# Attention turns: heads evicted behind the copy of the logits, root behind the maximum, context copied earlier, q and k by ScalarE

## What is computed

```python
x = x + 0.5 * _L0_ffn_ref(_layernorm(x), gate_up_proj, down_proj, router_w)   # 8 experts, the best 2 of each token
x = x + _L0_attn_ref(_layernorm(x), conv_w, conv_b, wq, bq, ..., proj_w, proj_b)
x = x + 0.5 * _L0_ffn_ref(_layernorm(x), gate_up_proj, down_proj, router_w)

# in _L0_attn_ref
qkv = conv1d(xp, conv_w) + conv_b            # causal, 3 taps, 3 x 64 channels
q, k, v = split(qkv)                          # then blocks of 128 tokens
scores = einsum('bqhk,bshk->bhqs', qh * scale, kh)      # 8 heads of 64
attn = softmax(where(causal, scores, -1e9))
mha_out = einsum('bqhk,hko->bqo', einsum('bhqs,bshk->bqhk', attn, vh), wo) + bo
out = mha_out @ proj_w + proj_b
```

## Time and profile before

| | |
|---|---|
| median of 3 runs | 757.45 us (755.04 to 759.35) |
| the profiled execution | 758.16 us, span 756.4 us |
| first experts, 0 to 255 us | 255 us, PE busy 226.85, DVE 169.14, ACT 156.11 |
| attention, 255 to 545 us | 290 us, PE busy 259.04, DVE 215.47, ACT 217.55, POOL 190.40 |
| second experts and last sums, 545 to 756 us | 211 us, PE busy 179.05, DVE 136.07, ACT 117.60 |
| maxima of the 32 blocks | start from 261.7 to 531.6 us, one each 8.7 us |

### The profile page before, as it was taken

How to read it: one execution, slowest core, us unless ns; L and a number is a source line. 1 busy time by engine, 2 the same in 40 slices (tenths; PEclk the granted TensorE clock), 3 DMA queues, 4 the chain that set the end, 5 groups by cost and what they waited for, 6 DMA issues and landing times. The chain is left out here.

```text
span 756.4 us, 18879 instructions
## 1 busy us (share of the span) xinstructions
PE 664.9 (88%) x5168; PEld 590.6 (78%) x5169; DVE 520.7 (69%) x1829; ACT 491.3 (65%) x1702; POOL 372.7 (49%) x418
## 2 busy tenths in 40 slices
PE   3999799999996699999898989978778999999854
PEld 3986699999993577878787878767557899999743
DVE  6588466666666467787878777858657677777653
ACT  5775566666664278887877868768444566666633
POOL 4200544444424546657787877554545444444500
PEclk9999899999999789999999999999879999999968
DMA  9930345444442211111222221110224543443289
GB/s 307 304 128 10 106 141 151 143 126 133 129 111 83 77 36 36 50 42 52 77 64 64 71 72 60 33 58 22 88 89 122 160 134 120 130 127 125 71 315 351
DMA packets 60424, 85.50 MB, mean 113 GB/s; under 512 B 10032, under 2 KB 46387, under 8 KB 60340
## 3 DMA queue, kind: packets, MB, share of 16 engines
q1 hardware_dynamic: 47332, 49.73, 21.2%
q0 software_dynamic: 13008, 34.69, 14.6%
HBM read 45.77 MB, written 37.44 MB: 110 GB/s over the span
## 5 line engine op out<-in xcount | busy, mean ns | idle before, releaser
L1811 PE MATMUL CC<-w_hi,turned_parts 128*128 x568 | 175.5, 351 | 3.6 <-issue 3.6
L725 POOL DMA_INDIRECT shared<-h_rows,tok_i x71 | 70.2, 988 | 116.4 <-issue 58.9
L1811 PEld LDWEIGHTS CC<-w_hi,turned_parts 128*128 128x128 f32 x568 | 105.4, 193 | 4.4 <-issue 4.3
L742 POOL DMA_INDIRECT y_rows<-shared,y_dest x71 | 70.0, 986 | 76.0 <-DVE y_dest L1349 57.8
L818 ACT ACTIVATE shared<-CC 128x176 f32<-128x176 f32 x142 | 45.2, 319 | 76.1 <-PE CC L1811 70.1
L1811 PE MATMUL CC<-w_lo,turned_parts 128*128 x284 | 93.3, 328 | 0.0
L934 ACT ACTIVATE pr<-SS,nmax 128x128 f32<-128x128 f32 x256 | 90.5, 401 | 0.5 <-DVE nmax L1542 0.5
L758 POOL TENSOR_TENSOR pr<-pr,prec 128x1024 f32<-128x1024 f32 x31 | 58.9, 1901 | 51.4 <-DVE prec L1572 50.2
L789 POOL DMA_INDIRECT h_regions<-h_store,dest x64 | 65.4, 1022 | 34.9 <-DVE dest L1436 18.4
L1330 DVE TENSOR_TENSOR shared<-shared,CC 128x176 f32<-128x176 f32 x142 | 48.0, 338 | 49.4 <-ACT shared L818 28.0
L766 POOL DMA_INDIRECT yg<-y_rows,slot_i x64 | 62.9, 983 | 34.5 <-DMA y_rows<-shared 15.5
(11 more groups left out here) (376 smaller groups left out, 2100.3 us busy)
## 6 DMA issues: line engine op xcount, KB each, us to landing
yg<-h_regions SPq DMA_DIRECT2D x71, 129.0 KB
y_rows<-shared SPq DMA_DIRECT2D x71, 128.0 KB
w_lo<-y_rows SPq DMA_DIRECT2D x9, 512.0 KB, 8.0
x_sb<-in_x_dram SPq DMA_DIRECT2D x8, 512.0 KB, 8.3
out_dram<-x_sb SPq DMA_DIRECT2D x16, 256.0 KB, 6.2
w_hi<-y_rows SPq DMA_DIRECT2D x7, 512.0 KB, 11.8
w_lo<-in_gupT_dram SPq DMA_DIRECT2D x2, 1408.0 KB, 11.1
shared<-tile_oh SPq DMA_DIRECT2D x32, 64.0 KB
```

The source lines that it names most:

```text
L725: pool.indirect_dma_start(out=rows[:, s % RING, 0:D], out_offset=None, in_=h_dram[:, :], in_offset=bass.IndirectOffsetOnAxis(ap=tok_i[:, s ...
L742: pool.indirect_dma_start(out=y_dram[0:TOPK * TOKENS, :], out_offset=bass.IndirectOffsetOnAxis(ap=y_dest[:, s:s + 1], axis=0), in_=y_sb[:, ...
L1811: i = pe.matmul(CC[:, 512 * (u % 2):512 * (u % 2) + GU], rows_part[:, u % 2, c * P:(c + 1) * P], weights, start=(n == 1), stop=(n == 3 * DC))
```

## The change

On DVE the order of a turn changes. The root goes from ahead of the maximum to behind it (up to turn 31). The copy of the context, `context(b)`, moves into `add_context`, between the addition to x and its statistics. The eviction of the head products moves from behind the reciprocal to directly behind the copy of the logits. A pick of four blocks moves from ahead of `add_context` to behind the eviction; smaller picks move behind `add_context`. The copy of q and k moves from DVE to ACT, where it stands behind the copy of `vo` and ahead of that of `hT`. On PE the ranks of a pick of four blocks move from the end of their turn into the next turn, behind the convolution of v and ahead of the scores.

```diff
@@ -863,6 +863,11 @@
                     a.activation(SS[:, :].rearrange("p (h s) -> p h s", s=P), mask_heads[:, :, :], ACT.Copy
                                  ).then_inc(t["exp"], 1)
 
+                def queries(p):
+                    a.wait_ge(t["conv"], 2 * p + 1)
+                    a.activation(qk[p % 2], B[:, 0:2 * P], ACT.Identity, bias=convb_sb[:, 0:1], scale=1.0
+                                 ).then_inc(t["qk"], 1)
+
                 def turned_pair(p):
                     a.wait_ge(t["xT"], 2 * p + 2)
                     a.activation(pair_of_rows(xT_hi, p), two_turned(), ACT.Copy).then_inc(t["xT_hi"], 2)
@@ -880,6 +885,7 @@
                                          scale=arstd[:, q:q + 1]).then_inc(t["normed"], 1)
                         if p == 0:
                             turned_pair(0)
+                            queries(0)
 
                 def turned(i):
                     if i == 0:
@@ -907,6 +913,8 @@
                     if there(i - 1):
                         a.wait_ge(t["vo"], i)
                         a.activation(vo[:, (u - 1) % 2, :], F[:, :], ACT.Copy).then_inc(t["vo_sb"], 1)
+                    if qk_pair(i) is not None:
+                        queries(qk_pair(i))
                     if there(i - POST):
                         b = i - POST
                         a.wait_ge(t["hrT"], b + 1)
@@ -1493,15 +1501,9 @@
                     sums(2, 1, 0)
                     turned_low(-2)
                     sums(3, 1, 1)
-                    queries(0)
                     root_of(moments[:, 1, :, :], 4, 2)
                     sums(4, 1, 0)
                     evict(-1)
-
-                def queries(p):
-                    v.wait_ge(t["conv"], 2 * p + 1)
-                    v.tensor_tensor(qk[p % 2], B[:, 0:2 * P],
-                                    convb_sb[:, 0:1].to_broadcast([P, 2 * P]), ALU.add).then_inc(t["qk"], 1)
 
                 def root(i):
                     root_of(moments[:, (i - 1) % 2, :, :], i - FIRST_RSTD + 1, 1)
@@ -1520,10 +1522,17 @@
                     v.scalar_tensor_tensor(out=shift[:, :], in0=m[:, :, 0], scalar=-1.0, in1=arstd[:, :],
                                            op0=ALU.mult, op1=ALU.mult).then_inc(t["rstd"], more)
 
+                def context(b):
+                    v.wait_ge(t["mha"], b + 1)
+                    v.tensor_tensor(mhaT[:, :], F[:, 0:P], mha_bias[:, 0:1].to_broadcast([P, P]), ALU.add
+                                    ).then_inc(t["mhaT"], 1)
+
                 def add_context(i):
                     b, u = i - 2, i % GROUP
                     v.wait_ge(t["out"], b + 1)
                     st.did(v.tensor_tensor(x_tile(b), x_tile(b), G[:, 0:D], ALU.add))
+                    if there(i - 1):
+                        context(i - 1)
                     st.wait()
                     v.sem_inc(t["res"], 1)
                     st.did(v.bn_stats(astats[:, 1, :], x_tile(b)))
@@ -1533,35 +1542,34 @@
 
                 def turn(i):
                     u = i % GROUP
-                    if qk_pair(i) is not None:
-                        queries(qk_pair(i))
-                    if i > 0 and (there(i + COMBINE - 1) or there(i - 3)):
+                    if i >= TILES and there(i - 3):
                         root(i)
                     if there(i):
                         v.wait_ge(t["scores"], i + 1)
                         v.tensor_reduce(nmax[:, u % 2, :], SS[:, :].rearrange("p (h s) -> p h s", s=P), AX.X, ALU.max,
                                         negate=True).then_inc(t["max"], 1)
-                    if i == 0:
+                    if there(i):
                         root(i)
                     if v_pair(i) is not None:
                         v.wait_ge(t["vhi"], v_pair(i) + 1)
                         v.tensor_tensor(vst_lo[:, :, :].rearrange("p b n -> p (b n)"), B[:, 2 * P:4 * P],
                                         vst_hi[:, :, :].rearrange("p b n -> p (b n)").bitcast(F32), ALU.subtract
                                         ).then_inc(t["qkv"], 1)
-                    if i in PICKS and i <= TILES:
-                        if PICKS[i][1] < 4:
-                            compare(*PICKS[i])
-                        pick(*PICKS[i])
                     if placed(i, False):
                         place(*placed(i, False))
                     if there(i - 2):
                         add_context(i)
+                    if i in PICKS and i <= TILES and PICKS[i][1] < 4:
+                        compare(*PICKS[i])
+                        pick(*PICKS[i])
                     if there(i - POST):
                         copy_logits(i - POST)
-                    if there(i - 1):
-                        v.wait_ge(t["mha"], i)
-                        v.tensor_tensor(mhaT[:, :], F[:, 0:P], mha_bias[:, 0:1].to_broadcast([P, P]), ALU.add
-                                        ).then_inc(t["mhaT"], 1)
+                    if there(i + 1):
+                        evict(i)
+                    if i in PICKS and i <= TILES and PICKS[i][1] == 4:
+                        pick(*PICKS[i])
+                    if there(i - 1) and not there(i - 2):
+                        context(i - 1)
                     if there(i + 3):
                         turned_low(i)
                     if there(i + COMBINE):
@@ -1576,8 +1584,6 @@
                             v.tensor_tensor(pr[:, u % 2, :, :], pr[:, u % 2, :, :],
                                             prec[:, u % 2, :].unsqueeze(2).to_broadcast([P, NH, P]),
                                             ALU.mult).then_inc(t["norm"], 1)
-                    if there(i + 1):
-                        evict(i)
                     if there(i + COMBINE):
                         b = i + COMBINE
                         st.did(v.bn_stats(astats[:, 0, :], x_tile(b)))
@@ -1931,6 +1937,8 @@
                         convolve_qk(qk_pair(i))
                     if i > 0 and v_pair(i) is not None:
                         convolve_v(v_pair(i))
+                    if i - 1 in PICKS and PICKS[i - 1][1] == 4:
+                        ranks(i - 1)
                     if there(i):
                         if i == 0:
                             for half in range(2):
@@ -2011,7 +2019,7 @@
                         for n, (part, weights) in enumerate(((vst_hi, wvo_hi), (vst_hi, wvo_lo), (vst_lo, wvo_hi))):
                             x = pe.matmul(F[:, :], part[:, u % 2, :], weights[:, :], start=(n == 0), stop=(n == 2))
                         x.then_inc(t["vo"], 1)
-                    if i in PICKS and i < TAIL_TURN:
+                    if i in PICKS and i < TAIL_TURN and PICKS[i][1] < 4:
                         ranks(i)
 
                 def ranks(i):
```

## The result

The changed kernel takes 786.12 us (median of 4 runs, 783.79 to 792.24), the kernel before 756.92 on the same chip (755.04 to 759.35). The ratio is 1.0396, with a 95% interval of 1.033 to 1.0463. The forecast was 777, with a range of 764 to 789; the measured time lies inside that range, 1 us above the 770 to 785 that the forecast gave as its own. The profiled execution took 785.68 us with a span of 783.9; before it was 758.16 and 756.4.

A forecast was written before the change was run, and what follows sets the result against it. The prediction took a ring of waits through projection, addition to x, reciprocal and POOL's multiplication as the bound. Added: +12.8 (turns 9 to 24), -1, +3.3, +2, +3, in all +20 on 757.45; forecast 777 us, range 764 to 789.

The forecast's parts named there:

- The ring: Attention turn: transposes, projection, addition to x, DVE's work up to the reciprocal, POOL's multiplication; 7.91 us in an even turn.
- T: Start of PE's transposes in a turn, 2.24 us after DVE's reciprocal in turn 20 and 2.56 in turn 19.
- 6.7 us from the transposes to the reciprocal: Sign of being right, in even turns of the attention: this stretch takes 6.7 us instead of 5.67.
- about 1.1 us for PE G: Sign of being right: DVE waits this long for PE's projection ahead of the addition to x in even turns.
- 8.95, about 9.0: Even turn's forecast length in us: 7.91 plus 0.56 for the eviction and 0.48 for the context's copy.
- "9.0" for the place: Turn with a place: it fits in the remaining wait ahead of the addition to x; 9.0 us against 8.49.
- 8.8: Odd turn's forecast length in us: 8.20 plus 0.61, from 0.56 eviction and 0.25 context copy, less 0.2.
- the 0.2 taken back for an earlier T: Odd turns: 0.2 us deducted because the bank of the convolution of q and k is free earlier.
- Cost 0: Copy of q and k on ACT: 0.39 us expected, fitting ACT's idle time ahead of the transposes' copy.
- 10.9: Pick turn's forecast length in us: 8.8 plus the pick's full 2.13 standing in the ring, against 9.95 before.
- the rival of the lower clock: PE's idle time brings the lower clock oftener: six more such turns, +10 us, 785 to 795; chance 0.13.
- The rival in which it gets faster: PE itself is the bound, earlier work closes its holes: 1.5 us off five pick turns, -7.5, 750; chance 0.07.

The follow-up runs named there:

- a_evict_back: Changed kernel with the eviction of the head products behind the reciprocal again; ratio 1.0151 to the kernel before.
- a_context_back: Changed kernel with the copy of the context behind the copy of the logits again, ahead of the eviction; ratio 1.029 to the kernel before.
- b_queries_act: Kernel before with only the copies of q and k moved from DVE to ACT; ratio 1.0017 to the kernel before.
- a_root_back: Changed kernel with the root ahead of the maximum again; ratio 1.0373 to the kernel before.
- a_experts_in_wait: Changed kernel with the two experts' rows moved from ahead of the reciprocal to just ahead of the addition to x; ratio 1.0335 to the kernel before.
- b_rec_early_root: Kernel before with the experts' rows behind reciprocal and eviction, and the root behind the maximum; ratio 1.0483 to the kernel before.
- b_rec_early: Kernel before with the experts' rows moved behind the reciprocal and the eviction; ratio 1.0478 to the kernel before.
- b_evict_early: Kernel before with only the eviction moved directly behind the copy of the logits, ahead of the context's copy; ratio 1.0401 to the kernel before.

## Why the prediction was right

**The ring.** Right, and shown by a_evict_back and a_context_back: what is put between the addition to x and the reciprocal is paid in full, and taken out again it comes back. T follows the reciprocal of an even turn by 2.24 us in both kernels. "6.7 us from the transposes to the reciprocal" was 6.74, "about 1.1 us for PE G" was 1.11.

**The terms.** "8.95, about 9.0" for the even turn: 8.98. "9.0" for the place: 8.98. "8.8" for the odd turn: 8.96; the part between T and reciprocal grew by 0.83 as forecast (0.81), but of the 0.2 taken back for an earlier T only 0.07 came. In turn 19 T is 439.62, 2.49 us behind the reciprocal, where it was 2.56 before. The operand of the convolution, the low part, stands 1.74 us ahead of the reciprocal in both kernels (415.89 and 417.63, 436.09 and 437.83), as the prediction had it. But the same operand holds T (4.23 us behind it in turns 17 and 19), so the bank that is free earlier gives nothing. "Cost 0" for q and k fits these sums, which leave no room for a cost, but in b_queries_act, without the other parts, the same move made the even turn 0.5 us longer: no run shows why, and none isolates it in the changed kernel.

**The pick.** "10.9" was mis-sized: 10.52. The 2.13 us of the earlier trace rows were read as the pick's own price. What follows its first row there, and POOL beside it (timelines of the kernel before, turn 21):

```profile
443.13 0.17 DVE L1400 TENSOR_REDUCE pick<-oh 128x4 f32<-128x32 f32 x1
443.33 0.42 DVE L1401 TENSOR_TENSOR rank<-pick,erank 128x32 f32<-128x32 f32 x1
...
442.62 0.56 POOL L776 TENSOR_SCALAR shared<-x_sb,arstd,shift 128x256 f32<-128x256 f32 x1
443.17 0.55 POOL L782 TENSOR_SCALAR h_store<-x_sb,arstd,shift 128x256 f32<-128x256 f32 x1
```

In the changed kernel, turn 17, where POOL is not at work on x:

```profile
425.12 0.15 DVE L1407 TENSOR_TENSOR h_store<-y_row,zeros 128x4 f32<-128x4 f32 x1
425.19 0.18 DVE L1408 TENSOR_REDUCE pick<-oh 128x4 f32<-128x32 f32 x1
425.40 0.19 DVE L1409 TENSOR_TENSOR rank<-pick,erank 128x32 f32<-128x32 f32 x1
```

Two of the pick's small operations, that of the earlier trace rows and L1401, took 0.51 and 0.42 us beside POOL's two normalisations, and 0.15 and 0.19 apart from them. Moved, the pick costs 1.55 us (425.12 to 426.67): 8.96 + 1.55 = 10.51. The other pick operations took about the same in both places.

**The sum.** Four turns were forecast at +3.2 and came at +2.9; the odd turn was taken 0.16 us too short and the pick turn 0.38 too long, so part of the agreement is luck. Turns 2 to 8 gave +5.25 (forecast 5.3), turns 9 to 24 +12.4 (11.8), turns 25 to 31 +5.0 (3). The attention is thus 22.7 against 20, and the missing part is mainly in the late turns. Turn 26 took 12.59 us, at a mean granted clock of 0.73, and turn 10 took 11.21 at 0.70, so both ran in part at the lower of PE's two levels (1.2 and 2.4 GHz); both follow a pick turn in which PE had been busy for over 10 us. The windows of turns 10 and 26, and of turn 26 in a_root_back:

```profile
350.55:361.76 11.21, 8.98 (x53) 7.06 (x54) 6.67 (x25) 7.09 (x26) 6.96 (x7) 0.70 0.15 48
504.25:516.84 12.59, 9.03 (x53) 7.17 (x53) 6.82 (x25) 7.09 (x26) 6.89 (x7) 0.73 0.12 43
...
495.96:504.95 8.99, 5.90 (x53) 4.82 (x54) 7.28 (x25) 6.98 (x26) 5.77 (x6) 1.00 0.09 30
```

In the kernel before, the same kind of turn fell to 0.84 and 0.83 (turns 10 and 22) and took 9.59 and 9.61 instead of 8.49. So the two disturbed turns add an estimated (11.21 + 12.59 - 2 x 8.98) - (9.59 + 9.61 - 2 x 8.49) = 3.6 us. That is the rival of the lower clock, in small: not oftener, but deeper. Emptier turns alone did not bring it: turns 14, 18 and 22 are of the same kind, PE was busy for only 5.9 us of each, and the clock was 1.00. And a_root_back, whose turns 16 to 19 are those of the changed kernel within 0.02 us, kept 1.00 in turn 26; its turns 25 to 31 are 65.4 us, only 0.8 above the kernel before, where the changed kernel's are 5.0 above. So most of the extra time in the late turns seems to belong to that one profile and not to a term of the sum. What makes the clock fall in one such turn and not in the next stays open. The rival in which it gets faster counts five pick turns, of which there are six: -9 instead of -7.5 us, which touches nothing else.

**Off by the rest.** The measured difference is 29 us, the turns explain 23. Ahead of turn 1 and behind turn 31 the profile has +2.4 each. Neither is shown to come from the change, by profiles of chips of the same speed. Ahead of turn 1, a_experts_in_wait has the changed kernel's code and took 276.12 us, where the changed kernel took 278.64 and the kernel before 276.21. Behind turn 31, b_rec_early_root and b_rec_early have the code of the kernel before and took 220.9 and 215.9 us, the changed kernel 220.3 and the kernel before 217.9. The sum had no term for these 4.8 us, nor for a deeper fall of the clock. So the turns brought the forecast within 9 us, and it is in part the width of the range that holds 786.

**The rule for the fullest engine.** The Trainium skill, Perfetto Trace Analysis, sections "Identifying the Most-Contended Engine" and "Optimization Strategy", would have one take the engine of the highest occupancy and make what it waits for start sooner. PE was the fullest at 88%. Its context did come earlier (T + 3.48 instead of T + 3.73 in even turns), and so did its heads (T + 4.40 instead of T + 5.79), and the kernel became 4% slower. That rule did not hold here, as the ring said.

## What to carry to other kernels

Where several engines pass one token round, find the ring before moving anything: follow one turn from an instruction back to itself, and sort each engine's work into what lies on that way, which is paid in full, and what lies in a wait, which is free. An early start for a consumer that isn't late is paid by everything queued behind it. Costs of moves don't add, when two of them share a wait. And an instruction's duration belongs to its place: the experts' rows, with two operands in SBUF, took 2.31 us beside POOL's multiplication and 1.00 us elsewhere.

## What the runs showed of the hardware

SBUF is the on-chip memory of the tiles, PSUM that of the banks (SS, CC, F, G, A and B here). DVE's instructions with two operands in SBUF were held off until the end of a POOL instruction that reads SBUF: the experts' rows (128x256) ended 0.80 us after POOL's instruction, whether that was the multiplication of 1.90 us or the copy of 1.04. The root's first operation, 0.15 to 0.19 us where nothing held it, took 0.78 us in 12 turns of b_evict_early and ended with POOL's multiplication. DVE, then POOL:

```profile
445.32 0.78 DVE L1511 SCALAR_TENSOR_TENSOR at<-arstd 128x2 f32<-128x2 f32 x1 [0.60 <-ACT arstd L906]
...
444.19 1.90 POOL L758 TENSOR_TENSOR pr<-pr,prec 128x1024 f32<-128x1024 f32 x1 [0.97 <-DVE prec L1574]
```

Not held were the eviction, one operand of which is in a PSUM bank (0.64 us beside the multiplication in the kernel before, 0.68 without it in the changed one), and the statistics with one operand (0.42 to 0.43). It goes both ways: POOL's second normalisation took 0.74 us beside the experts' rows, and 0.55 without. The Trainium skill, SBUF — State Buffer, section "Who interferes with whom", says that a DVE instruction with two SBUF inputs contends with a GpSimd instruction that reads SBUF, and that one with at most one SBUF input, outside the two-port modes, does not; by that rule the trace agrees in each of these cases.

ACT's copy of q and k out of bank B with the bias took 0.47 us (16 of them, 468 ns on average), where the prediction had taken the 0.39 of v's plain copy from the same bank.
